# An audio-tower layer with an attention that keeps its scores twice, turned and unturned, and divides on the output

## What is computed

```python
h = patches(x) @ W.T + b            # 5 frames of 23 -> 115 inputs, 121 rows per batch
h = batch_norm(relu(h)) * gamma + beta                    # over all 32*121 = 3872 rows
n = layernorm(h)                                          # D = 128
q, k, v = n @ q_w.T + q_b, n @ k_w.T + k_b, n @ v_w.T + v_b      # 8 heads of 16
scores = q @ k.T / 4 + col_bias    # per batch and head 121 x 121; bias per key from edges
h = h + (softmax(scores) @ v) @ o_w.T + o_b
n = layernorm(h)
e = argmax(n @ Wr + br)                                   # one of 8 experts per row
h = h + relu(n @ W1[e] + b1[e]) @ W2[e] + b2[e]           # 128 -> 512 -> 128
```

## Time and profile before

| | |
|---|---|
| median of 3 runs | 346.77 us (345.53 to 349.64) |
| profiled execution | 345.34 us, span 343.6 us |
| busy, share of the span | PE 275.7 us (80%), PEld 215.0 (63%), DVE 225.4 (66%), ACT 227.0 (66%), POOL 213.2 (62%) |
| HBM read / written | 10.69 MB / 8.44 MB |
| DMA, mean over the span | 56 GB/s |

### The profile page before, as it was taken

One profiled execution on the slowest core, in us unless ns is written; L12 is line 12 of the kernel. 1 busy time (PEld: TensorE's weight loads), 2 busy tenths in 40 slices (PEclk: granted clock), 3 DMA queues, 4 the chain that ended last, 5 costly groups with the idle time before them and its releaser, 6 DMA issues. The chain is left out here.

```text
span 343.6 us, 7885 instructions
## 1 busy us (share of the span) xinstructions
PE 275.7 (80%) x2139; PEld 215.0 (63%) x2139; DVE 225.4 (66%) x714; ACT 227.0 (66%) x843; POOL 213.2 (62%) x299
## 2 busy tenths in 40 slices
PE   3890969899999998897898879856008999999980
PEld 2660746556767665665656656545007999999970
DVE  2895676888988999877787686455403565656540
ACT  3851378889888998697897788640005777777740
POOL 7044554787766867888888886667721454545551
PEclk9995698999999999999999999895557999999996
DMA  3200990000000000001000100112634333333300
GB/s 94 79 2 1 303 281 18 0 2 1 3 0 2 1 3 15 16 15 32 15 24 23 31 15 17 30 31 73 171 98 122 93 101 109 94 104 108 91 13 0
DMA packets 15579, 19.15 MB, mean 56 GB/s; under 512 B 3960, under 2 KB 11676, under 8 KB 15537
## 3 DMA queue, kind: packets, MB, share of 16 engines
q1 hardware_dynamic: 11520, 11.73, 12.1%
q0 software_dynamic: 3296, 5.98, 6.0%
q10 hardware_dynamic: 720, 0.94, 0.9%
HBM read 10.69 MB, written 8.44 MB: 56 GB/s over the span
## 5 line engine op out<-in xcount | busy, mean ns | idle before, releaser
L467 ACT ACTIVATE P<-psS,nmax 121x121 f32<-121x121 f32 x256 | 88.9, 380 | 17.9 <-DVE nmax L709 17.2
L929 PE MATMUL psS<-patT,qT 128*121 128x484 f32 x128 | 64.3, 607 | 2.5 <-ACT P L467 1.7
L396 POOL DMA_INDIRECT out<-y_out,xg x38 | 36.9, 971 | 46.9 <-issue 31.5
L362 POOL TENSOR_TENSOR P<-P,rden 121x968 f32<-121x968 f32 x31 | 56.5, 1823 | 8.2 <-DVE rden L781 7.6
L467 ACT ACTIVATION_READ_ACCUMULATOR P<-psS,nmax 121x1 f32 x256 | 57.4, 224 | 0.0
L835 DVE TENSOR_SCALAR hT<-psT,b1T 128x128 f32<-128x128 f32 x76 | 23.3, 347 | 46.7 <-PE psT L1062 46.6
L709 DVE TENSOR_REDUCE nmax<-psS 121x4 f32<-121x484 f32 x64 | 41.5, 651 | 15.0 <-PE psS L929 15.0
L941 PE MATMUL psT<-ident,P 121*121 121x121 f32 x256 | 34.4, 277 | 15.2 <-POOL P L362 13.2
L941 PEld LDWEIGHTS psT<-ident,P 121*121 121x121 f32 x256 | 29.7, 185 | 21.9 <-POOL P L362 19.2
L374 POOL DMA_INDIRECT region_d<-rows,pos x32 | 34.9, 1091 | 8.8 <-issue 8.8
L476 ACT ACTIVATE PT<-psT 121x968 f32<-121x968 f32 x32 | 32.0, 1000 | 12.6 <-PE psT L941 12.6
(11 more groups left out here) (210 smaller groups left out, 620.4 us busy)
## 6 DMA issues: line engine op xcount, KB each, us to landing
xg<-region_d SPq DMA_DIRECT2D x38, 128.5 KB
W_sb<-in_L_ffn_W SPq DMA_DIRECT2D x1, 2048.0 KB, 9.2
region_d<-pads SPq DMA_DIRECT2D x11, 128.5 KB, 4.3
out<-y_out,xg POOLq DMA_INDIRECT x38
region_d<-pads ACTq DMA_DIRECT2D x4, 128.5 KB
b_bc<-in_L_ffn_b SPq DMA_DIRECT2D x1, 512.0 KB, 5.9
region_d<-rows,pos POOLq DMA_INDIRECT x32
xs<-in_x ACTq DMA_DIRECT2D x1, 402.5 KB, 3.9
```

Of the source, the lines that this page charges most:

```text
L362: pool.tensor_tensor(P[0:L, i % 2, :, :], P[0:L, i % 2, :, :], rden[0:L, i % 2, :].unsqueeze(2).to_broadcast([L, H, L]), ALU.mult).then_in ...
L396: pool.indirect_dma_start(out, bass.IndirectOffsetOnAxis(xg[:, u, 2 * D:ROW].bitcast(I32), 0), y_out[:, u, :], None, bounds_check=N - 1, o ...
L467: ins = act.activation(P[0:L, t % 2, h, :], psS[0:L, h // HG, h % HG * L:(h % HG + 1) * L], ACT.Exp, bias=nmax[0:L, h:h + 1], accum_out=de ...
L929: pe.matmul(psS[0:L, g, 0:HG * L], qT[:, t // 2 % 2, g, t % 2 * L:t % 2 * L + L], kbd[:, t % 4, g, :], start=True, stop=True).then_inc(s_S, 1)
```

## The change

In words:
- **Scores twice.** For each of the 8 heads `scores` makes a matmul of 32 partitions of queries and of keys, 121 x 121, with head j of a group in bank j of psS (four banks, psT is gone). `scores_T` makes the same products once more with keys and queries exchanged, so that the result lies turned. Before that the negated maximum is turned on PE (nT) and added to the queries (`qm` on DVE) in a row of the padding which meets a one in the keys, so that the turned scores come out with the maximum already subtracted. The block-diagonal keys, the eight transposes of P and the copy to PT fall away.
- **Two exponentials** of 121 x 484 in place of eight of 121 x 121, one for banks 2 and 3, one for banks 0 and 1; the maximum is taken of banks 0 and 1 while the first exponential reads 2 and 3, then they change places (waits on s_exp and s_max).
- **Division on the output.** V gets a column of ones, so the product also holds the sums. The output is turned back (`OTs`, L1013), divided (rden, `on`), turned again (L1007) and multiplied with owX. `normalize` on POOL is gone.
- **Wider rows.** h0 is produced by a matmul with idX = [Wr centred, identity minus mean, mean], 137 columns, so a row holds the router's logits, the centred row and the mean; owX carries the output weights the same way. The second norm is a sum of squares (DVE, `sq2`), var and the power on POOL, the scaling on ACT (`rows`, x2) and the logits on DVE (`lg`); the turning of rows and the matmul with Wr are gone. h0k has two buffers.
- **Pads** are written once at fixed places by two DMAs before the scatters. The last tile of an expert starts earlier where its rows run out, and rows that it reads again are masked (`again`, `mask`, `sidx`).
- STEPS is B + 6; the expert groups at the end are of two batches, and the scatter of a batch stands 8 or more steps behind its scores.

The core of the diff, with lines left out:

```diff
+WX = E + D + 1
+ROW = 2 * D + 2
+GROUPS = tuple((b, 4) for b in range(0, B - 8, 4)) + tuple((b, 2) for b in range(B - 8, B, 2))
 NG = len(GROUPS)
...
-            for n in range(XT):
-                sp.dma_start(region_d[E * CAP + n * 128:E * CAP + (n + 1) * 128, :], pads[:, :]).then_inc(d_extra, 16)
-
-            write_pads(sp, range(0, E // 2))
+            sp.dma_start(region_d[0:E * CAP, :].rearrange("(e r) c -> r e c", r=CAP)[0:128, :, :],
+                         pads[:, :].unsqueeze(1).to_broadcast([128, E, ROW])).then_inc(d_pads, 16)
+            sp.dma_start(region_d[E * CAP:E * CAP + XT * 128, :].rearrange("(n r) c -> r n c", r=128),
+                         pads[:, :].unsqueeze(1).to_broadcast([128, XT, ROW])).then_inc(d_pads, 16)
...
-            def normalize(i):
-
-                pool.wait_ge(s_rd, i + 1)
-                pool.tensor_tensor(P[0:L, i % 2, :, :], P[0:L, i % 2, :, :],
-                                   rden[0:L, i % 2, :].unsqueeze(2).to_broadcast([L, H, L]), ALU.mult).then_inc(s_Pn, 1)
...
+                pool.wait_ge(a_ob, 1)
+                pool.tensor_tensor(rows[0:L, 2 * p:2 * p + 2, 0:WX], h0k[0:L, p % 2, :, :],
+                                   ob_bc[0:L, :].unsqueeze(1).to_broadcast([L, 2, WX]), ALU.add).then_inc(s_h0b, 1)
...
+                pool.wait_ge(s_sq2, b + 1)
+                pool.tensor_scalar(var2[0:L, c], ss2[0:L, c], 1.0 / D, EPS, ALU.mult, ALU.add).then_inc(s_v2, 1)
                 pool.wait_ge(s_v2, b + 1)
-                pool.tensor_tensor(rs2[0:L, b % 2:b % 2 + 1], var2[0:L, b % 2:b % 2 + 1], minus_half[0:L, 0:1], ALU.pow).then_inc(s_r2, 1)
...
+                pool.tensor_tensor(rs2[0:L, c], var2[0:L, c], minus_half[0:L, 0:1], ALU.pow).then_inc(s_r2, 1)
...
-            for t in range(B + 4):
-                if has(t, 1) and t != B:
-                    normalize(t - 1)
-                if t % 2 == 1 and t // 2 + 2 < NP:
-                    norm1(t // 2 + 2)
-                if has(t, 3):
-                    rstd2(t - 3)
-                if t >= 16 and t < B + 3:
-                    scatter_rows(t - 16)
-            for b in range(B - 13, B):
+            pool.wait_ge(s_rowid, 1)
...
+            for t in range(STEPS):
+                p = t // 2
+                if t == 8:
+                    pool.wait_ge(d_pads, 32)
+                if t % 2 == 1 and t > 1 and p + 2 < NP:
+                    biased_rows(p + 2)
+                while done < B and scatter_step(done) <= t and done <= t - 8:
+                    scatter_rows(done)
+                    done += 1
+                if t % 2 == 0 and t > 0 and p + 2 < NP:
+                    norm1(p + 2)
+                if has(t, 4):
+                    rstd2(t - 4)
+            for b in range(done, B):
...
-                    for h in range(H):
-                        if h % HG == 0:
-                            act.wait_ge(s_max, 2 * t + 1 + h // HG)
-                        ins = act.activation(P[0:L, t % 2, h, :], psS[0:L, h // HG, h % HG * L:(h % HG + 1) * L],
-                                             ACT.Exp, bias=nmax[0:L, h:h + 1], accum_out=den[0:L, t % 2, h:h + 1])
-                        if h % HG == HG - 1:
-                            ins.then_inc(s_exp, 1)
...
+                if has(t, 5):
+                    b = t - 5
+                    act.wait_ge(s_r2, b + 1)
+                    act.activation(rows[0:L, b, WX:WX + D], rows[0:L, b, E:E + D], ACT.Identity,
+                                   scale=rs2[0:L, b % 4:b % 4 + 1]).then_inc(s_x2, 1)
...
+                    act.activation(PT[0:L, (t - 1) % 2, 2:4, :, :], score_half(1, 1), ACT.Exp).then_inc(s_exp, 1)
+                if has(t, 4):
+                    act.wait_ge(s_OT, t - 3)
+                    act.activation(oT[:, :], psO[:, 256:256 + L], ACT.Identity).then_inc(s_oT, 1)
...
+                    if has(t, 0):
+                        act.wait_ge(s_max, 2 * t + 1)
+                    act.activation(PT[0:L, (t - 1) % 2, 0:2, :, :], score_half(1, 0), ACT.Exp).then_inc(s_exp, 1)
...
+                if has(t, 2):
+                    act.wait_ge(s_PV, t - 1)
+                    act.activation(OTs[:, :, :], psO[:, 0:256].rearrange("p (a n) -> p a n", a=2)[:, :, 0:L],
+                                   ACT.Identity).then_inc(s_OTs, 1)
...
+                    dve.wait_ge(s_S, t + 1)
+                    if t > 0:
+                        dve.wait_ge(s_ST, t)
+                    for pair in range(2):
+                        if pair == 1 and t > 0:
+                            dve.wait_ge(s_exp, 2 * t - 1)
+                        dve.tensor_reduce(nmax[0:L, pair * 64:pair * 64 + 64].rearrange("p (j c) -> p j c", c=HB)[:, :, HD + 1:HD + 3],
+                                          score_half(0, pair), AX.X, ALU.max, negate=True).then_inc(s_max, 1)
...
+                    dve.wait_ge(s_r2, b + 1)
+                    dve.scalar_tensor_tensor(out=lg[0:L, b % 8, :], in0=rows[0:L, b, 0:E], scalar=rs2[0:L, b % 4:b % 4 + 1],
+                                             in1=br_bc[0:L, :], op0=ALU.mult, op1=ALU.add).then_inc(s_lg, 1)
                 if has(t, 0):
-                    row_max(t, 1)
-                if not rows_first:
-                    logits()
+                    dve.wait_ge(s_nT, t + 1)
+                    dve.tensor_tensor(qm[:, :, :], qT[:, p % 2, :, t % 2 * L:t % 2 * L + L],
+                                      psU[:, 0:L].unsqueeze(1).to_broadcast([128, 2, L]), ALU.add).then_inc(s_qm, 1)
...
+                    dve.wait_ge(s_bT, t - 2)
+                    turned = psU[0:L, 258:258 + 226].rearrange("p (a c) -> p a c", a=2)
+                    dve.reciprocal(rden[0:L, :].rearrange("p (a j) -> p a j", a=2), turned[:, :, HD:HD + 3 * HB + 1:HB]).then_inc(s_rd, 1)
+                    dve.wait_ge(s_rd, t - 2)
+                    for a in range(2):
+                        ins = dve.tensor_tensor(on[0:L, a * HG * HD:(a + 1) * HG * HD].rearrange("p (h c) -> p h c", c=HD),
+                                                psU[0:L, 258 + a * 113:258 + a * 113 + 128].rearrange("p (j c) -> p j c", c=HB)[:, :, 0:HD],
+                                                rden[0:L, a * HG:(a + 1) * HG].unsqueeze(2).to_broadcast([L, HG, HD]), ALU.mult)
+                    ins.then_inc(s_on, 1)
...
+                    dve.tensor_tensor(rows[0:L, b, 0:WX], psU[0:L, 121:121 + WX], rows[0:L, b, 0:WX], ALU.add).then_inc(s_h1, 1)
...
+                    dve.scalar_tensor_tensor(out=sq2[0:L, b % 2, :], in0=rows[0:L, b, E:E + D], scalar=1.0, in1=rows[0:L, b, E:E + D],
+                                             op0=ALU.mult, op1=ALU.mult, accum_out=ss2[0:L, b % 4:b % 4 + 1]).then_inc(s_sq2, 1)
+                for g in range(NG):
+                    if ranked(g) - 1 == t:
+                        expert_max(g)
+                        expert_rank(g)
+                        expert_onehot(g)
+                        expert_seen(g)
...
+            def scores(t):
+
+                p, n0 = t // 2, t % 2 * L
+                for a in range(2):
+                    for j in range(HG):
+                        rws = slice(j * HB, (j + 1) * HB)
+                        ins = pe.matmul(psS[0:L, j, a * 128:a * 128 + L], qT[rws, p % 2, a, n0:n0 + L],
+                                        kT[rws, p % 2, a, n0:n0 + L], start=True, stop=True)
+                ins.then_inc(s_S, 1)
+
+            def scores_T(t):
+
+                p, n0 = t // 2, t % 2 * L
+                for a in range(2):
+                    for j in range(HG):
+                        rws = slice(j * HB, (j + 1) * HB)
+                        ins = pe.matmul(psS[0:L, j, 256 + a * 128:256 + a * 128 + L], kT[rws, p % 2, a, n0:n0 + L],
+                                        qm[rws, a, :], start=True, stop=True)
+                ins.then_inc(s_ST, 1)
...
+            pe.wait_ge(a_wts, 7)
+            pe.matmul(banks[4][:, 0:WX], proj_in[:, 3, :], idX[:, :], start=True, stop=True).then_inc(a_owp, 1)
+            pe.wait_ge(a_vbm, 2)
+            pe.wait_ge(a_owx, 1)
+            pe.matmul(banks[5][0:L, 256:256 + WX], vb_mat[:, 0:L], owX[:, :], start=True, stop=False)
...
+            pe.wait_ge(s_xT, 2)
+            pe.wait_ge(s_h0k, 3)
...
+                if has(t, 2):
+                    pe.wait_ge(s_exp, 2 * t - 2)
                 if has(t, 0):
+                    if t > 0:
+                        pe.wait_ge(s_max, 2 * t)
                     if even:
-                        pe.wait_ge(s_kbd, 2 * p + 2)
...
+                    scores(t)
+                if has(t, 1):
+                    pe.wait_ge(s_qm, t)
+                    scores_T(t - 1)
+
+                if has(t, 4):
+                    pe.wait_ge(s_on, t - 3)
+                    if has(t, 3):
+                        pe.wait_ge(s_OTs, t - 2)
+                    pe.transpose(psO[:, 256:256 + L], on[0:L, :], ident[0:L, 0:L]).then_inc(s_OT, 1)
+                if has(t, 5):
```

(21 more changed lines are left out.)

650 lines of the change are left out of this document (297 added, 353 removed).

## The result

The changed kernel takes 328.59 us (median of 4 runs, 327.06 to 332.18) against 347.3 for the kernel before (median of 4 runs, 345.53 to 349.64): ratio 0.944, interval 0.936 to 0.952. The changed kernel's profiled execution takes 329.08 us and spans 326.6, that of before 345.34 and 343.6.

What follows compares the result with a forecast made beforehand. ACT and PE fill the first stretch; POOL, ACT and PE share the second. 345.34 - 16.5 (tail) - 6.6 (loop) + 4.4 (start) = 326.6, said as 327; forecast's own range 318 to 336, overall 311 to 358.

Steps and rivals of the forecast that it cites:

- Tail: From last output row to first tile load: 9.7 us against 26.2, two scatters left and pads gone; gain 16.5.
- the table of row places is covered: Tail: table on DVE, about 5 us, runs beside two scatters and their landing, 5.5; uncovered perhaps 1 us.
- Loop: 31 batch intervals: 23 at 5.57 and eight at 4.35, 162.9 us against 169.5; gain 6.6.
- the ring: Loop: POOL's power, ACT's row scaling and exponential, DVE's second maximum to sum of squares, power again; 5.0 us, mean 5.57.
- in-between rival: Loop: score sets partly packed or PE's clock falling now and then; 335 to 352 us, middle 342; chance 0.13.
- PE: PE's work in the loop: 4.0 us a step if row groups pack, up to 6.4 if weight loads queue.
- Queueing rival: Loop: weight loads queue, scores and turned scores take 1.76 each, PE has 6.4 a step; 368 us; chance 0.18.
- rest of PE's step: 2.85: Loop, PE without scores: PV 0.55, transposes and output matmul 0.8, projections, values, h0 and xn 1.4, ranking 0.1.
- Its threshold: Loop: queueing decides from about 1.1 us per set of eight, where PE passes 5.2 of the ring; 338 at 1.2.
- Shorter ring: Loop: early row scaling leaves DVE's 4 us and its wait for nT, 4.6 a step; 305 us; chance 0.07.
- Start: Before the loop: first scores at 43.9, 3.3 late, another 1.1 until the output row; loss 4.4, bounds 1 to 7.

Runs made afterwards that it cites:

- the two kernels above: Each against the changed kernel: scatters 16 steps behind their batch, 338.7 us; eight pad writes in SyncE's queue ahead of the tile loads, 338.2 us.
- with the ring open: Changed kernel with ACT's row scaling for the second norm moved behind the step's two exponentials: 295.8 us, ratio 0.852 to the kernel before.
- the kernel with early keys: Changed kernel with row scaling behind the exponentials and DVE's key copy right behind the two maxima: 290.7 us, ratio 0.834 to the kernel before.
- The kernel with sets of 1.8 us: Changed kernel with each whole set of eight score and eight turned score matmuls repeated four times: 394.5 us, ratio 1.122 to the kernel before.
- The kernel with sets of 1.08: Changed kernel with each score and turned score matmul issued twice in a row: 335.0 us, ratio 0.966 to the kernel before.
- the kernel with four in a row: Changed kernel with each score and turned score matmul issued four times in a row: 662.9 us, 641.75 in the profiled execution.

## Why the prediction was right, step by step

I said 327; it is 328.6. That it is so near is in part luck. The terms start from the profiled execution of before, 2.0 below its median, and give 326.6 for that of the changed kernel, which took 329.1, 0.5 above its median. Of the missing 2.5, tail and loop make 0.7 and 0.8 and the start takes 0.35 back; another 1.3 lie where I had put nothing: from the first tile load to the end it is 87.6 us against 87.0, and the part outside the span is 2.5 us and not the 1.7 that was taken over. The terms, one by one:

- **Tail**, 9.7 us: measured 10.4. From the last output row to the first of the two scatters it is 5.15 us where I had 4.2: the addition of the row itself (0.33) was left out, and POOL starts the scatter 0.88 behind the end of `pos`, where I had 0.2 for all hand-overs. The scatter before it on POOL ends with `pos`, within 0.03 us, so by these rows a shorter choice of experts would have gained 0.5 at most (a gap of 0.31 between scatters in place of 0.84); that four scatters and not two come behind the last output row, the prediction did not see. From there to the tile load it is 5.2, forecast 5.5. That the table of row places is covered was right but narrow, 0.6 us. That scatters and pads are both needed for it, which the prediction said only by naming both, is shown by the two kernels above; that the earlier `pos` and fewer scatters left are part of the gain is in its sum but not in its words.
- **Loop**, 162.9: measured 163.7. Steps forecast as 5.0, 5.85 and 6.42 are 4.83, 5.84 and 6.47, the last eight 4.49 on the mean where I had 4.35. The members of the ring were right, with one correction: parallel to the second maximum, oT and the output matmul close it too, so that by these rows a faster maximum alone would not have helped (not run). Moving L484, which both branches have in common, took 32.5 us off, and that shows that the ring was the bound and not only present. Two steps of 31 are 0.7 longer (5.57 and 5.50 for 4.83), where the granted clock, the third number from the end, falls:

```profile
90.00:95.00 5.00, 4.33 (x63) 3.50 (x63) 3.17 (x13) 2.12 (x6) 1.14 (x3) 0.77 0.01 3
...
135.00:140.00 5.00, 4.33 (x60) 3.60 (x61) 3.08 (x13) 2.20 (x7) 1.90 (x4) 0.71 0.09 25
```

  The in-between rival, a clock that falls now and then, was thus real, and cost 1.4 us and not 15.
- **PE**, 4.0 a step: with the ring open PE's steps without a wait or a ranking are 3.98. Over all of the first 23 steps it is 4.25, in the kernel with early keys, where PE is busy 39.8 of 40 us. A set costs 0.52 and not 0.55. Here lay the prediction's one real uncertainty. The Trainium skill, page "TensorE: Matmul & The Clock Gate", section "LDWEIGHTS (loading the stationary operand)", says that fewer rows don't make a weight load shorter, which by itself leaves the 1.76 a set that the loads' rows give. Its part "Packing small matmuls — row/col tiling" has a factor of 3.07 for four row groups at 512 moving columns, by which I estimate 1.76 / 3.07 = 0.57. The measured 0.52 is near the second and not near the first.
- **Queueing rival**, 368: it did not happen, but had it, my price was too low. The kernel with sets of 1.8 us takes 394.5. The step that failed in it is "rest of PE's step: 2.85". It is right where PE has no other wait (3.98 - 1.04 = 2.9), but in every second step of that kernel PE waits for oT (0.31) and the keys (0.36, with a ranking 0.67), ranking is 0.51 in every fourth step, 0.13 a step and not 0.1, every fourth set takes 2.4, and the first row came 11.5 later and not 3.
- **Its threshold**, 1.1 us a set: for steps without a first norm it is 0.96, for the others above 1.08. The prediction's own terms give PE 2.2 + 2.85 = 5.05 there and not 5.2, and its 338 for sets of 1.2 does not follow from them: two times 0.1 in 31 steps is 6 us, 333. The kernel with sets of 1.08 takes 335.0, most of that in the first steps.
- **Shorter ring**, 305 and 0.07: in the changed kernel it did not happen. The kernel that opens the ring takes 295.8. The step that failed in the rival is DVE's 4 us and its wait for nT, 4.6: with the ring open, steps are 3.98 and 4.5, and 5.24 with a ranking, DVE is busy 33.5 of 40 us in 100 to 140, and its waits lie within PE's work.
- **Start**, first scores 43.9, output row 4.4 late: measured 43.90, and 64.96 against 60.91, 4.05 late.

## What to carry to other kernels

When a change takes work off every engine and the time hardly moves, look for a wait that starts in one batch and ends in another: add the members of the ring through the in-order queues, and ask which of them could stand behind what it holds up. Here one copy on ACT, needed only by a scatter steps later, stood ahead of the exponentials and cost 33 of 328 us. Where two queues end at nearly the same place, look at both before mending one: here each old cost alone brought back more than half of what both had cost.

## What the runs showed of the hardware that I had not expected

- Row groups of 32 rows pack, in f32: eight matmuls of 32x121 take 0.52 us and their sixteen weight loads 0.42, where sixteen passes of 121 columns would take 2.0 by the long score matmul of before (0.125 each). The order decides: 0.065 us a matmul in a single set and 0.056 over four whole sets, in which successive ones differ in row group, 0.067 when two in a row share it, 0.14 when four do. Why two and four differ by so much I can't say from these runs, nor whether it is the row group or the bank of psS, which changes with it.
- In the kernel with four in a row, PE is busy 92% of the span and the granted clock is 0.79 on the mean, down to 0.61 in 400 to 440 us; with whole sets, it is the same matmuls and the clock at 1.00 from 60 to 180. A PE busy by the profile did not keep its clock there: from 128.2 to 136.2 us it is busy without a gap at a granted clock of 0.50, and a set takes 7.9 us where it takes 4.2 to 4.4 at 1.00.
- POOL's two xn instructions (L351, L353) take 0.38 us each, against 0.51 for their like before, with one column to multiply by (and the constant 0 to add), where those before added one column and multiplied by another. No kernel differs in that alone.
